# Four block layers on one core: the projections' small matmuls as 64x64 quarters, factors of two tiles at a time, and values gated later

## The reference

```
xg = group_norm(x)                         # 32 groups of 2 channels
h  = layer_norm(xg) * w + b                # over the 64 channels of each pixel
v  = (h @ Wp + bp) * sigmoid(h @ Wg + bg)  # gated values: 64 (layer 1) or 128 (layers 2, 3) channels
og = sigmoid(h @ Wo + bo)                  # output gate, layers 2 and 3 only
z  = einsum over a pixel axis of the halves of v
x  = x + projection(layer_norm(z)) with its gate
```

## Time and profile before

| | us |
|---|---|
| median of three runs | 1943.2 (1935.28 to 1946.1) |
| the profiled execution | 1933.59 |
| its span in the trace | 1931.8 |
| granted TensorE clock, mean | 0.938 of full speed |
| TensorE busy | 1538.0 (80%) |
| VectorE busy | 1331.0 (69%) |
| ScalarE busy | 882.9 (46%) |
| projection stage, layer 1 | about 336 to 517 |
| projection stage, layers 2 and 3 | about 756 to 997 and 1320 to 1559 |

### The profile page before, as it was taken

The page is one execution under the profiler, slowest core; times in us unless marked ns, Lnnn a source line. Parts: engine busy times, 40 slices in busy tenths (PEclk is TensorE's granted clock), DMA queues, the critical chain, the costliest instruction groups (busy, mean ns, idle before and its releaser), DMA issues. The chain is left out here.

```text
span 1931.8 us, 29873 instructions
## 1 busy us (share of the span) xinstructions
PE 1538.0 (80%) x7296; PEld 758.3 (39%) x7296; DVE 1331.0 (69%) x2126; ACT 882.9 (46%) x1446; POOL 265.5 (14%) x224
## 2 busy tenths in 40 slices
PE   5597498966586576999979995667999967766998
PEld 4445233211275122222239992222222235652447
DVE  3884499067588696377757776993577757767994
ACT  3795343833234244766646662005666634440003
POOL 0000087000000484100000001661100000000000
PEclk8998799999898798999989997998999989997999
DMA  5667410035567440098889995870388879976759
GB/s 201 212 132 220 128 47 13 5 108 142 157 214 261 100 89 3 11 309 280 279 274 299 304 302 183 289 280 1 129 288 279 282 250 307 309 252 228 273 211 348
DMA packets 253817, 386.36 MB, mean 200 GB/s; under 512 B 24227, under 2 KB 165414, under 8 KB 244262
## 3 DMA queue, kind: packets, MB, share of 16 engines
q1 hardware_dynamic: 205718, 337.35, 54.2%
q10 hardware_dynamic: 48016, 47.98, 7.5%
HBM read 193.74 MB, written 190.32 MB: 199 GB/s over the span
## 5 line engine op out<-in xcount | busy, mean ns | idle before, releaser
L993 PE MATMUL bank<-work 128*128 128x256 f32 x1408 | 346.8, 394 | 59.0 <-ACT work L1025 31.8
L719 ACT ACTIVATE work<-bank,bias 128x512 f32<-128x512 f32 x448 | 276.9, 686 | 210.8 <-PE bank L617 135.4
L1345 POOL TENSOR_TENSOR xT<-xT,work 128x512 f32 (+1 forms) x192 | 241.9, 1270 | 846.6 <-DVE work L1399 846.5
L784 DVE SCALAR_TENSOR_TENSOR work<-bank,bias,work 128x512 f32<-128x512 f32 x320 | 228.4, 747 | 138.3 <-PE bank L650 94.7
L993 PEld LDWEIGHTS bank<-work 128*128 128x128 f32 x1408 | 265.1, 197 | 113.6 <-issue 23.2
L650 PE MATMUL bank<-work,w 64*128 64x512 f32 x1024 | 268.8, 627 | 5.4 <-DVE work L784 4.0
L1018 ACT COPY work<-bank 128x512 f32<-128x512 f32 x176 | 103.2, 586 | 230.0 <-PE bank L993 129.1
L706 ACT ACTIVATE work<-bank,fold 128x512 f32<-128x512 f32 x192 | 116.7, 689 | 190.3 <-PE bank L617 190.0
L1284 PE MATMUL bank<-work,w 128*128 128x512 f32 (+2 forms) x512 | 193.3, 612 | 1.3 <-DVE work L1362 1.3
L1273 PE MATMUL bank<-work,sel 128*128 128x512 bf16 x176 | 70.1, 403 | 151.0 <-DMA work<-rstd_parts 98.2
L1082 DVE TENSOR_TENSOR work<-work 128x512 f32<-128x512 f32 x176 | 121.2, 689 | 70.8 <-ACT work L1018 70.1
(11 more groups left out here) (131 smaller groups left out, 1834.7 us busy)
## 6 DMA issues: line engine op xcount, KB each, us to landing
work<-hidden_rows SPq DMA_DIRECT2D x352, 256.0 KB, 3.6
hidden_rows<-work SPq DMA_DIRECT2D x288, 256.0 KB, 2.2
z_rows<-work ACTq DMA_DIRECT2D x176, 256.0 KB, 3.6
work<-z_rows SPq DMA_DIRECT2D x32, 1024.0 KB
work<-gate_rows SPq DMA_DIRECT2D x32, 1024.0 KB, 4.8
work<-in_x SPq DMA_DIRECT2D x64, 256.0 KB, 3.9
hidden_rows<-work SPq DMA_DIRECT2D x128, 128.0 KB, 2.3
gate_rows<-work SPq DMA_DIRECT2D x64, 256.0 KB, 2.4
```

The source lines that it names most:

```text
L719: nc.scalar.activation(result(tile, column), GB[(NG * j + n) % len(GB)][:, :], ACT.Sigmoid, bias=bias(name)).then_inc(gate_sb, 1)
L784: dve.scalar_tensor_tensor(out=r, in0=VB[(NV * j + m) % len(VB)][:, :], scalar=bias(value_w), in1=r, op0=ALU.add, op1=ALU.mult).then_inc(v ...
L993: mm = pe.matmul(ZB[b % 2][:, r * N:r * N + N], a[:, kk, r * P:r * P + P], x[:, kk, :], start=(kk == 0), stop=(kk == 1))
L1345: pool.tensor_tensor(x, x, term[:, ring(j, q, TERMS), :], ALU.add).then_inc(x_sb, 1)
```

## The change

It does five things, all of them in `project` and its constants.

1. `both_halves` issues each 64x128 matmul as two of 64x64, so that gates and values of the stacked layers run in quarters as well.
2. `factors(t)` takes the place of `factor`: the factors of tiles t (from partitions 0 to 63 of `parts`) and t+1 (from 64 to 127), each as two 64x64 quarters, with eight new selection matrices (`SEL_IN`) beside the old ones. `LEAD` is now 2 instead of 3: normed runs two tiles ahead, and the prologue norms four tiles instead of three.
3. The rows in which variances stand (`place`, `window`) and the layout of `parts` are changed to suit.
4. The copies into `parts` have 8 rows instead of 16, and are 24 for each x instead of 12.
5. VectorE gates values `VALUE_LAG` tiles behind: one in the stacked layers, two in layer 1; and it now gates ahead of norming.

The core of the diff:

```diff
-NSEL = JP + SETS[2] + SETS[4]
+NSEL = JP + SETS[2] + SETS[4] + JP // 2
...
-    LEAD = 3
+    LEAD = 2
+    VALUE_LAG = 1 if stacked else 2
...
-            def factor(t, g, j):
-                if t in (0, JP // 2):
-                    pe.wait_ge(parts_in[t // (JP // 2)], 16 * 12)
...
-                at_least(pe, h_sb, t - 1)
-                pe.matmul(FAC[j % 2][:, :], core.sel[:, SEL[1] + j, :],
-                          parts[:, j // (JP // 2), g, :], start=True, stop=True).then_inc(fac_mm, 1)
+            def factors(t):
+                if t in (0, JP // 2):
+                    pe.wait_ge(parts_in[t // (JP // 2)], 16 * 24)
+                if t == 0:
+                    pe.wait_ge(sd_sb, 1)
+                at_least(pe, h_sb, t)
+                for n in range(2):
+                    q, j = (t + n) // JP, (t + n) % JP
+                    x, r, i = place(j)
+                    rows = slice(C * r, C * r + C)
+                    sel = core.sel[rows, SEL_IN + 4 * (q % 2) + i, :]
+                    for side in (lower, upper):
+                        mm = pe.matmul(FAC[n][side, :], sel[:, side], parts[rows, x, q // 2, :], start=True, stop=True)
+                    mm.then_inc(fac_mm, 1)
 
             def both_halves(outs, name, j, made):
                 for out, r in zip(outs, (lower, upper)):
-                    pe.matmul(out[:, :], w(name)[r, :], h[r, j % H, :], start=True, stop=True).then_inc(made, 1)
+                    for side in (lower, upper):
+                        mm = pe.matmul(out[side, :], w(name)[r, side], h[r, j % H, :], start=True, stop=True)
+                    mm.then_inc(made, 1)
...
-                for n in range(2):
-                    ahead(g, j + LEAD + n)
+                if not first and t + LEAD < NT:
+                    factors(t + LEAD)
...
-            factor(0, 0, 0)
-            factor(1, 0, 1)
+            factors(0)
             mean_squares(JP - 1)
-            factor(2, 0, 2)
+            factors(2)
...
             def pair(g, j):
-                tile(g, j)
-                tile(g, j + 1)
+                for n in range(2):
+                    t = g * JP + j + n
+                    if not isinstance(t, int) or t >= VALUE_LAG:
+                        gated(t - VALUE_LAG, (j + n - VALUE_LAG) % JP)
+                    if not isinstance(t, int) or LEAD <= t < NT - LEAD:
+                        normed(t + LEAD, j + n + LEAD)
...
                     for q in range(4):
-                        sp.dma_start(parts[32 * n + 16 * x:32 * n + 16 * x + 16, x, q, :],
-                                     three[32 * q + 16 * x:32 * q + 16 * x + 16, n, :]).then_inc(parts_in[x], 16)
+                        for r in range(2):
+                            first = C * r + 24 * (q % 2) + 8 * n
+                            rows = 32 * q + 16 * x + 8 * r
+                            sp.dma_start(parts[first:first + 8, x, q // 2, :],
+                                         three[rows:rows + 8, n, :]).then_inc(parts_in[x], 16)
```

More of the change, by code:

```diff
@@ L73, in constants @@
                         k[r, col:col + cz] = 1
+    for slab_half in range(2):
+        for i in range(4):
+            for h in range(2):
+                col = K_SEL + (SEL_IN + 4 * slab_half + i) * P + h * C
+                for r in range(2):
+                    for part in range(3):
+                        k[C * r + 24 * slab_half + 8 * part + 2 * i + h, col:col + C] = 1
     return k
@@ L581, in project @@
     three, at = core.area([3, T], at, BF16)
-    parts, at = core.area([2, NT // JP, T], at, BF16)
+    parts, at = core.area([2, NT // JP // 2, T], at, BF16)
     res, at = core.area([4, NG * T], at)
@@ L590, in project, with place @@
     stores = (NG, NG + 1)
+    def place(j):
+        return j // 8, j % 2, j % 8 // 2
     def pairs(loop, body):
@@ L599, in pairs @@
             body(groups - 1, j)
-    def exists(t):
-        return not isinstance(t, int) or t < NT
     with ExitStack() as ctx:
@@ L628, in mean_squares @@
                 for q in range(4):
-                    window = WIN * (q % 2) + 2 * (JP - 1 - s)
+                    x, r, i = place(s)
+                    window = WIN * (q % 2) + 2 * (JP - 1 - 8 * x - 4 * r - i)
                     mm = pe.matmul(STAT[s // 8][32 * q:32 * q + 32, :], core.summer[:, window:window + 32],
@@ L748, in _ @@
                 if x:
-                    pool.wait_ge(parts_in[0], 16 * 12)
+                    pool.wait_ge(parts_in[0], 16 * 24)
                 pool.tensor_copy(a, rec).then_inc(split, 1)
@@ L766, in normed @@
                 dve.wait_ge(fac_mm, t + 1)
-                if isinstance(t, int) and t < LEAD:
+                if isinstance(t, int) and t < 2 * LEAD:
                     dve.wait_ge(sum_mm, JP - 1)
-                if isinstance(t, int) and t == LEAD:
+                if isinstance(t, int) and t == 2 * LEAD:
                     dve.wait_ge(sum_mm, JP)
@@ L772, in normed, with gated @@
                                          in1=FAC[j % 2][:, :], op0=ALU.subtract, op1=ALU.mult).then_inc(h_sb, 1)
-            def tile(g, j):
-                t = g * JP + j
-                if exists(t + LEAD):
-                    normed(t + LEAD, j + LEAD)
+            def gated(t, j):
                 for m in range(NV):
@@ L787, in pair @@
             def pair(g, j):
-                tile(g, j)
-                tile(g, j + 1)
+                for n in range(2):
[4 more added lines that the diff above has]
+                        normed(t + LEAD, j + n + LEAD)
             dve.memset(parts, 0.0).then_inc(zeroed, 1)
             inverse(0)
-            for t in range(LEAD):
+            for t in range(2 * LEAD):
                 normed(t, t)
@@ L796, in _ @@
             pairs(dve.Fori, pair)
+            for t in range(NT - VALUE_LAG, NT):
+                gated(t, t % JP)
         @block.sync
```

8 lines of the change are left out of this document (2 added, 6 removed).

## The result

The changed kernel takes 1951.19 us (median of seven runs, 1946.01 to 1954.25), the kernel before 1940.18 in the seven runs beside it (1935.28 to 1947.63). The ratio is 1.0048, with an interval of 1.0025 to 1.0071: slower by about half a per cent. The forecast was 1943, no change; it was too low by 8 us. The time lies inside the range of 1916 to 1966.

What follows compares the result with a forecast made beforehand. Layer 1 was bound by a ring of TensorE and VectorE waits, stacked pairs by a chain through ScalarE and VectorE. Terms -28.6 - 15.1 + 38.7 + 3 + 1.7 = -0.3 us left 1943 us, range 1916 to 1966.

Steps and rivals of the forecast that it cites:

- forecast sum of zero: Whole kernel: gains of the periods against costs of starts, clock and constants, summing to -0.3 us.
- The start of each stage: Start of three projection stages: twice the copies at 0.629 us each delay the first store by 12.9, +38.7 us.
- lump of 3 us: Layers 2 and 3, after TensorE's new idle time: half clock costs about 1.5 us each, +3 us (0 to 10).
- Layer 1, the period: Layer 1 pairs: later gating shortens the period from 3.76 to 2.70 us over 27 periods, -28.6 us (-30 to -16).
- the ring of the stores: Layer 1: a sigmoid waits for the store four tiles back; three periods at least 8.06 us, one 2.69.
- The stacked period: Pairs of layers 2 and 3: period 5.35 us, 0.28 less, over twice 27 periods, -15.1 us (-21 to 0).
- The third rival: Stacked layers gain nothing: queued stores or late gated(t) keep the period at 5.63; +15 us, 1958; chance 11%.
- The chain's reason: Stacked pair: ScalarE's third sigmoid, ending at 2.92, releases VectorE at 2.97; the values are ready by 2.86.
- The constants: Loads ahead of everything: eight more selection matrices, 512 KB, +1.7 us (2.9 if the larger load goes at its own pace).
- Cheap copies (0.45): SyncE queue at stage starts: 8-row copy 0.41 us and a gap of 0.04, 25 us less, 1918 us; chance 27%.
- The dear ones (0.81): SyncE queue at stage starts: 8-row copy 0.77 us and a gap of 0.04, adds 25 us, 1968; chance 14%.
- the 38% for no change: Whole kernel: chance of a time within 0.5%, 35 from the forecast and 3 from the third rival.

Runs made afterwards that it cites:

- e11: The changed kernel with eight result tiles instead of four in layer 1: 1940.38 us, ratio 1.0023 to the kernel before.
- e10: As e1, with eight result tiles instead of four in layer 1: 1892.86 us, ratio 0.9777 to the kernel before.
- e6: The kernel before with only the later gating (one tile in stacked layers, two in layer 1): 1907.3 us, ratio 0.9856.
- e1: The changed kernel with factors, copies, layout and constants of before; quarters and later gating stay: 1900.02 us, ratio 0.9805 to the kernel before.
- e5: The kernel before with only the 64x128 matmuls of gates and values issued as 64x64 quarters: 1924.25 us, ratio 0.9947.
- e4: The changed kernel with half of the copies, those for the odd tiles, issued by GpSimd: 1905.0 us, ratio 0.9823 to the kernel before.
- e7: As e1, with 6 of the 12 16-row copies for each x issued by GpSimd: 1890.34 us, ratio 0.9781 to the kernel before.
- e2: The changed kernel with the copies of the odd tiles' factors left out (24 instead of 48): 1906.91 us, ratio 0.9831 to the kernel before.
- e8: As e1, with all 12 16-row copies of the second x issued by GpSimd: 1906.49 us, ratio 0.9852 to the kernel before.

## Why the prediction was wrong

The two directions and the places were as the prediction said, and so was the mechanism, but for a second hold at the start that it did not name. Two sizes were far off, both to the same side, and the forecast sum of zero was a difference of two large terms that had no room for that.

**The start of each stage, the step that failed most.** The prediction's term of 12.9 us per stage measured 15.7, 16.1 and 15.6: 47.4 instead of 38.7. In layer 2 (from the first copy, the same points as in the prediction):

| | forecast | measured |
|---|---|---|
| factors landed, VectorE norms | +4.7 | +6.2 (normed(0) at 805.95 - 787.57 against 805.62 - 793.46) |
| second set of copies begins | +5.4 | +7.55 (813.77 - 787.57 against 812.11 - 793.46) |
| first store | +12.9 | +16.06 |

The price of a copy is the larger part. I took the time of a 16-row copy and its gap (0.629), and it was 0.665: 1.4 us by the end of the first set (the first entry is longer too), 1.0 in the second. The smaller part, the 0.7 that is left, is a step that I had not followed. I let the last sums of squares move with the wait, but not get slower, and they run at the half clock behind it (1.93 us instead of 1.07; the granted clock from 804 to 808 us is 0.50, where it was 1.00 before), with the factors of tiles 2 and 3, the reciprocal and the second set behind them. The cost of the half clock was in the sum as a lump of 3 us, not at the place where it is on the path to the first store.

The chain of this term had one path, the first store. The runs show two. The factors of tile 8 come free 43.0 us after the first copy in layer 1, and e11, which takes the stores' hold away there, gives back only 3.5 of the 15.7. The prediction also read layer 1 like layer 2, where a store had released the fifth tile; in layer 1 before, TensorE did, after 5.17 us of waiting for the copies. The sum did not suffer, since both paths run through the same queue.

**Layer 1, the period: mis-sized.** I made the ring of the stores the longest, at 2.69, from a median landing of 2.3 us, and took 2.70. The mean was 2.86. The 3.76 of before was off as well: it is one pair's period, put in for all 27. The last two of them took 2.58 each in the kernel before, since there is nothing left to norm, and the mean was 3.68. So the 27 periods took 77.3 us instead of 99.3, a gain of 22.1 instead of 28.6 us. A ring that is computed at the median landing and comes out just above VectorE's 2.64 is exceeded whenever a landing is late (the second of a tile's two stores landed after 2.3 us in the median and 4.0 at most, over the three stages), and gives nothing back when one is early. e10 and e11 show it: with the ring twice as long the holds are gone and the period is VectorE's. The rest of this term was right, and e6 showed that the later gating alone makes it: 2.77. The 0.09 by which the changed kernel is above e6 and e1 are the two periods behind the hold of 1.65 us, where the granted clock fell to 0.65; what set that hold off no run shows.

**The stacked period: right.** 5.37 us against 5.35 (the mean over 24 periods from 841.09 to 970.02 is 5.37 too), with every point of the chain within 0.02. Over the last 27 periods of each stage the gain was 6.5 and 6.3 us, -12.8 instead of -15.1, since the mean of before was 5.60 and 5.61 over them and not 5.63. e5 showed that the quarters alone make it (5.36), e1 that the paired factors add nothing. The third rival, that the stores hold it at 5.63, is out: they went at 296 GB/s. The chain's reason was half right. At 876.36 the profile names the values (L665) as VectorE's releaser, while ScalarE's third sigmoid ended only at 876.30 (874.45 + 2 x 0.58 + 0.69), so the two were last together. No run took one of them away.

**The constants: right.** The loads land at 12.75 us instead of 11.03, +1.7.

With the measured sizes: -22.1 (layer 1) - 12.8 (layers 2 and 3) + 47.4 (starts) + 1.7 (constants) = +14.2. The stages and loads gave +13.4; the rest of the stages was shorter by the difference. They leave no room for the lump of 3 us for the half clock beside them: what the half clock cost is in the 47.4, some 0.7 us in each stage.

**The rivals on the copies.** Cheap copies (0.45) are out. The dear ones (0.81) are out as well, and their threshold was too high: I put the decision for slower at 0.70 per copy, on a sum of -0.3. With the periods and the clocked-down sums right it would have been near 0.645: -22.1 - 12.8 + 38.7 + 2.1 (three times the 0.7) + 1.7 = +7.6 at 0.629, and 2.1 more over 141 copies is 0.015. The copy measured 0.665. The range held; the 38% for no change stood on a sum to which both errors added.

The Trainium skill, page "DMA: Bandwidth & Descriptors", section "Why a DMA increments its semaphore by 16 and not by 1", has the sequencer write the missing increments of a transfer that runs on fewer than 16 engines. The 8-row copy is 0.035 us dearer than the 16-row one, as such a write would make it, but the 4-row copy (0.584), which by that rule has more to make up, is not. GpSimd's queue shows a like step, 0.518 us at 8 rows (e4) against 0.484 at 16 (e7), so it is not SyncE's alone. The runs do not bear the rule out as the cause of the 0.035. They do not rule it out either: by an estimate from the three medians on SyncE's queue, 0.010 us for a row and 0.115 for a write of any size would give all three.

## What to carry to other kernels

Count the entries in a queue, not their bytes, and follow both what stands behind them in it and what waits for the last of them to land. Here cutting every copy in two doubled the time of a set of them; the first store and the factors of the second half both came some 16 us later. Taking one of the two holds away gives little back (e7, e11); shortening the queue itself gives back nearly all (e2), and sending half of the copies through GpSimd's idle queue does that without dropping one (e4). Before a faster inner loop is paid for with longer preparation, look at which queue the preparation runs in, and undo the parts one by one: two of the three parts here were worth 2%, and the third took them back.

A ring whose length at median times comes out at the bound of another engine is not hidden. Take the spread of the landings into the period, or lengthen the ring; eight tiles instead of four took 4.4 us off layer 1 here (e10).

## What the runs showed of the hardware that was not expected

- The issue of a small SBUF-to-SBUF copy on the SyncE queue does not depend on its rows in a steady way: 0.589 us for 16 rows, 0.624 for 8, 0.584 for 4 (1 KB in each row), minima and medians equal to within 7 ns for the last two. I had bounded the 8-row copy with lines through a single row at 0.253 and 16 rows at 0.589, which would have made it 0.41.
- The same 8-row copy takes 0.518 us on GpSimd's queue (e4, median of 72), less than on SyncE's.
- In e8 the 16-row copies took 0.487 us each from GpSimd but landed only after 2.8 us (median), where they landed after 1.8 from SyncE. The shorter issue was given back by the landing. When only six were issued in a row (e7), they took 0.484 and landed after 1.9.
